# Adapter-conditioned feed-forward layer on one core: the order of the first loads, the bias copy and the steps of side work in the opening stage

## The reference

```python
# conditioning: one low-rank adapter (rank 16) for each of 8 batches, chosen by itok
Bx   = einsum('bni,bri->bnr', x, cond_B[itok])       # x: 8 x 512 x 2048, float32
cond = einsum('bnr,bor->bno', Bx, cond_A[itok])
# feed-forward on cond
base   = einsum('bsi,oi->bso', cond, base_w) + base_b    # base_w: 2048 x 2048
hid    = einsum('bsi,ri->bsr', cond, ffn_A)              # ffn_A: 64 x 2048
probs  = softmax(einsum('bsi,ei->bse', cond, router_w))  # 16 experts
combine = one-hot of the top 2, weighted and normalized
delta  = einsum('bse,bsr,eor->bso', combine, hid, ffn_B) # ffn_B: 16 x 2048 x 64
out = x + base + 0.5 * delta
```

## Time and profile before

| | before |
|---|---|
| median of 3 runs | 472.77 us (472.57 to 473.4) |
| the profiled execution | 471.14 us, of which the span from first to last instruction is 468.9 us |
| TensorE busy | 414.8 us, 88% |
| VectorE busy | 298.5 us, 64% |
| moved by DMA | 135.31 MB, 289 GB/s over the span |
| mean granted TensorE clock | 0.981 of full speed |

### The profile page before, as it was taken

One profiled execution on the slowest core, in us unless ns is written; L12 is line 12 of the kernel. 1 busy time (PEld: TensorE's weight loads), 2 busy tenths in 40 slices (PEclk: granted clock), 3 DMA queues, 4 the chain that ended last, 5 costly groups with the idle time before them and its releaser, 6 DMA issues.

```text
span 468.9 us, 6167 instructions
## 1 busy us (share of the span) xinstructions
PE 414.8 (88%) x2240; PEld 278.2 (59%) x2240; DVE 298.5 (64%) x699; ACT 108.9 (23%) x166; POOL 48.2 (10%) x54
## 2 busy tenths in 40 slices
PE   0056879998988999999999999999999999999996
PEld 0045767777755566566556755655665566566675
DVE  1587249795636666757775677667567766767353
ACT  0011231425543432023002301310230132123210
POOL 3332000001200012002001200120120012002000
PEclk9999778999999999999999999999999999999999
DMA  8999999969997998899889989998997999655844
GB/s 201 202 359 343 353 358 365 297 189 355 296 302 154 271 342 303 290 291 370 293 282 328 335 273 293 369 323 270 293 363 264 293 336 325 241 192 180 300 170 180
DMA packets 97876, 135.31 MB, mean 289 GB/s; under 512 B 14068, under 2 KB 50932, under 8 KB 97844
## 3 DMA queue, kind: packets, MB, share of 16 engines
q1 hardware_dynamic: 67380, 102.07, 66.2%
q10 hardware_dynamic: 30466, 32.84, 24.0%
HBM read 99.24 MB, written 35.65 MB: 288 GB/s over the span
## 4 chain that ended last, share of the span: by engine, by line
PE 70%; DVE 11%; DMA 8%; ACTq 6%; issue 2%; ACT 1%; SPq 0%; DVEq 0%
PE ps L858 13%; PE ps L875 12%; PE ps L876 10%; PE ps L877 10%; PE ps L823 7%; PE ps L888 7%; PE ps L878 5%; DMA bexpT<-in_x 4%; DMA early_u<-in_L_ffn_B 4%; PE ps L813 4%; DVE h_r L673 4%; DVE xT L692 4%; ACTq L293 3%; DVE xbuf L801 2%; ACTq L278 2%
## 5 line engine op out<-in xcount | busy, mean ns | idle before, releaser
L801 DVE TENSOR_TENSOR xbuf<-ps,xbuf 128x512 f32<-128x512 f32 x128 | 86.9, 679 | 105.6 <-PE ps L878 105.3
L875 PE MATMUL ps<-h_r,u_r 128*128 128x512 f32 x256 | 109.3, 427 | 9.2 <-DVE xbuf L801 9.2
L876 PE MATMUL ps<-h_r,u_r 128*128 128x512 f32 x256 | 100.3, 392 | 0.0
L877 PE MATMUL ps<-h_r,u_r 128*128 128x512 f32 x256 | 100.1, 391 | 0.0
L823 PE MATMUL ps<-early 128*128 128x256 f32 x256 | 66.8, 412 | 33.2 <-DVE early L611 28.5
L875 PEld LDWEIGHTS ps<-h_r,u_r 128*128 128x128 f32 x256 | 48.0, 188 | 50.2 <-issue 20.1
L823 PEld LDWEIGHTS ps<-early 128*128 128x128 f32 x256 | 50.8, 207 | 45.4 <-issue 29.7
L692 DVE STREAM_TRANSPOSE xT<-xbuf 128x512 f32<-128x512 f32 x112 | 72.0, 681 | 0.0
L858 PE MATMUL ps<-bexpT,cur 128*32 128x512 f32 x512 | 61.6, 598 | 2.1 <-DVE h_r L673 2.1
L633 DVE STREAM_TRANSPOSE early<-xbuf 128x256 f32<-128x256 f32 x128 | 47.4, 415 | 19.5 <-PE ps L823 11.1
L464 ACT ACTIVATE h_r<-ps 128x512 fp32r<-128x512 f32 x64 | 35.7, 594 | 86.7 <-issue 54.3
(11 more groups left out here) (64 smaller groups left out, 228.5 us busy)
## 6 DMA issues: line engine op xcount, KB each, us to landing
out<-xbuf SPq DMA_DIRECT2D x31, 1024.0 KB, 7.1
xbuf<-in_x SPq DMA_DIRECT2D x30, 1024.0 KB, 7.0
xbuf<-in_x SPq DMA_DIRECT2D x28, 512.0 KB, 8.4
xbuf<-in_x ACTq DMA_DIRECT2D x28, 512.0 KB, 9.5
xbuf<-in_L_ffn_base_w SPq DMA_DIRECT2D x16, 512.0 KB, 13.5
xbuf<-in_L_ffn_base_w ACTq DMA_DIRECT2D x16, 512.0 KB, 12.7
gm_r<-g_hilo SPq DMA_DIRECT2D x128, 32.0 KB, 6.1
early_u<-in_L_ffn_B SPq DMA_DIRECT2D x14, 256.0 KB, 11.3
```

Source lines behind the costliest of these rows:

```text
L801: dve.tensor_tensor(xs, ps[:, ACC + t % 2, :], xs, ALU.add).then_inc(s_out, 1)
L875: pe.matmul(acc, u_r[:, b.q, 0, h, tok_t], hi, start=(h == 0), stop=False)
L876: pe.matmul(acc, u_r[:, b.q, 0, h, tok_t], lo, start=False, stop=False)
L877: pe.matmul(acc, u_r[:, b.q, 1, h, tok_t], hi, start=False, stop=False)
```

## The change

A's loads are put among the four transfers of W's first piece on both queues. GpSimd waits for `take_a`'s last copy before it touches the bias. x of batch 0 is requested behind W's sixth piece and transposed in steps 76 to 98 (two blocks in three steps) instead of 44 to 89 (one block in three). The experts' steps move later, most of all the first four; the late ones go behind tiles 1, 2, 5 and 6 instead of 0, 2, 4 and 6. On both queues W's fifth piece goes ahead of expert group 2.

```diff
-        X_AT = {44 + 3 * j: j for j in range(KD)}
-        BX_AFTER = {66: 4, 92: 8}
-        SLOT_AT = {94: 8, 97: 9, 101: 10, 104: 11, 107: 12, 118: 13, 122: 14}
+        X_AT = {76 + 3 * j // 2: j for j in range(KD)}
+        BX_AFTER = {84: 4, 95: 8}
+        SLOT_AT = {97: 8, 100: 9, 104: 10, 107: 11, 110: 12, 119: 13, 123: 14}
-        E_AT = {20: 0, 26: 1, 34: 2, 40: 3, 52: 4, 60: 5, 70: 6, 78: 7, 95: 8, 102: 9, 109: 10, 117: 11}
-        E_LATE = {0: 12, 2: 13, 4: 14, 6: 15}
+        E_AT = {24: 0, 34: 1, 44: 2, 54: 3, 64: 4, 70: 5, 78: 6, 86: 7, 97: 8, 104: 9, 111: 10, 118: 11}
+        E_LATE = {1: 12, 2: 13, 5: 14, 6: 15}
-        E_FRESH, EIN_AT = 11, 94
-        PIECE_AT, X0_AT = {10: 4, 27: 5, 42: 6, 58: 7}, 26
+        E_FRESH, EIN_AT = 11, 97
+        PIECE_AT, X0_AT = {23: 5, 43: 6, 59: 7}, 29
...
-            load_w(sp, 0, (0, 1))
-            load_cond_a(sp, range(0, NAD // 2))
+            load_cond_a(sp, range(0, 1))
+            load_w(sp, 0, (0,))
+            load_cond_a(sp, range(1, 2))
+            load_w(sp, 0, (1,))
+            load_cond_a(sp, range(2, NAD // 2))
...
+            load_w(sp, 4, (0, 1))
             load_experts(sp, 2, 0)
-            load_w(sp, 4, (0, 1))
+            load_w(sp, 5, (0, 1))
             load_experts(sp, 3, 0)
+            load_x0(sp, (0, 1))
             load_experts(sp, 4, 0)
-            load_x0(sp, (0, 1))
-            load_w(sp, 5, (0, 1))
             load_experts(sp, 5, 0)
...
+            pool.wait_ge(s_a, NB)
             pool.wait_ge(s_bias, 32)
...
-            load_w(act, 0, (2, 3))
-            load_cond_a(act, range(NAD // 2, NAD))
+            load_cond_a(act, range(NAD // 2, NAD // 2 + 1))
+            load_w(act, 0, (2,))
+            load_cond_a(act, range(NAD // 2 + 1, NAD // 2 + 2))
+            load_w(act, 0, (3,))
+            load_cond_a(act, range(NAD // 2 + 2, NAD))
...
             load_experts(act, 1, 1)
+            load_w(act, 4, (2, 3))
             load_experts(act, 2, 1)
```

## The result

The changed kernel takes 479.56 us (median of 4 runs, 478.98 to 479.69) against 472.94 for the kernel before: ratio 1.0137, 95% interval 1.0119 to 1.0155. It is slower by 6.6 us where 3.8 us of gain were forecast. The profiled span is 477.5 us, 8.6 more than before; the profiled execution of the kernel before lay 1.6 us under its median, so differences between these two traces come out up to 2 us larger than those between the medians.

A forecast was written before the change was run, and what follows sets the result against it. It took TensorE as the busiest engine, with DMA feeding the stage up to 80 us. A lead of 3.3 us plus 0.5 from the late experts made 3.8 us: 469.0 us, range 465.0 to 473.9.

The forecast's parts named there:

- Part 1: Opening: GpSimd's bias after A shortens A's copies from 9.1 to 2.3 us; first product at 21.6 instead of 28.45.
- Part 2: A's loads among W's: A still lands at 19.1; 2 us later or earlier would be swallowed by the next wait.
- Part 3: Waits at expert groups 0 and 1: four steps (1.7 us) left of 6.8; TensorE at step 34 at about 47.7.
- Part 4: Steps 34 to 64: step 64 at 76, a lead of 15 steps, 6.5 us.
- its two limits: Step 64: TensorE's path with ScalarE's stand in x's issue until 52.6 gives 75.0; group 4's landing behind x gives 74.8.
- The slower rival: Group 4 lands late behind x and delays everything from step 64, at 82: 2.2 us slower, 475.0; chance 0.20.
- a sign of being wrong: At step 64: the prediction is wrong if expert group 4 lands after 80.
- Part 5: Dense x stretch, steps 76 to 98: VectorE sets it, second x product ends at 101.3, lead falls to 4.5 us.
- Part 6: Steps 97 to 127: logits at step 100 wait 1.2 us behind expert group 8, lead 3.3; the rest counts nothing.
- Part 7: Late experts among the tiles: h ahead of group 12's copy, new stalls between close flips; net gain 0.5 us.
- the real gain: Expert groups 0 and 1: more steps ahead of each load use idle time; step 34 at 47.7, before step 26.

The follow-up runs named there:

- b1: Kernel before with GpSimd's wait for the copies of A (bias after A) as its only change: ratio 0.9993.
- b2: Kernel before with A's loads among W's first piece as its only change: ratio 1.0091.
- a1: Changed kernel with A behind W's first piece again, as before: ratio 1.0083 to the kernel before.
- repaired kernel: Changed kernel with A behind W, the store of g's first part early, the routing earlier and group 5 ahead of W (d3): ratio 0.9968.
- f2: Repaired kernel (d3) with A among W's first piece again: ratio 1.0015.
- c2: Changed kernel with the late experts behind tiles 0, 2, 4 and 6 as before: ratio 1.0171.
- d1: c3 with the routing's parts 8 to 14 one or two steps earlier each: ratio 0.9975.
- f3: Repaired kernel (d3) with the store of g's first part behind expert groups 5 and 6 again: ratio 1.0024.
- c1: Changed kernel with the routing's part 8 at step 96 instead of 97: ratio 1.0145.
- f1: Changed kernel with the routing's parts one or two steps earlier: ratio 1.0102.
- c3: Changed kernel with A behind W and the store of g's first part ahead of expert groups 5 and 6: ratio 1.0028.
- d3: c3 with the routing earlier and expert group 5 ahead of W's seventh piece on ScalarE's queue: ratio 0.9968.
- f4: Kernel before with x requested late and transposed densely, and the routing's steps as in f1: ratio 1.0080.

## Why the prediction was wrong

**Part 1 held.** 1.71 us for the copies, the first product at 21.35 in b1 (21.6 predicted), the transposes at their old speed (14 in 6.08 us in b1, begun beside GpSimd's subtraction, 14 in 6.06 before). One reading was short: line 611 had three stretched copies, not one. Those of 1692 and 1983 ns ran beside the two casts of 1885 and 2042 ns, that of 4583 ns beside the subtraction; the earlier trace rows, which gives least, median and most, does not show the first two.

**Part 2 failed.** "I leave A's landing at 19.1": it moved to 21.7 to 22.1, and expert group 0 to between 42.6 and 43.3. I had let the next wait swallow a late A, but the same delay moves the loads behind A, and so that wait itself. Worth 4.3 us in the kernel before (b2), 2.6 in the changed one (a1), 2.2 in the repaired one (f2). Why A is late was not separated: the windows show 185 instead of 194 GB/s up to 20 us, and ScalarE's issues of A end at 16.14, SyncE's at 13.81, where before the two ended within 0.8 us of each other.

**Part 3 held** where A was not late: in b1 the 7 us are gone at group 0, and a1 has group 1 flipped at 47.86 for 47.7.

**Part 4's sizes were near, but of its two limits only one was met.** With A behind W, step 64 comes at 77.3 (a1) for 76, and group 4 lands at 75.2 for 74.8. TensorE does not wait there for group 4's load (at most 0.26 us, in c2): the time goes to ScalarE's stand in x's issue, as the part also had it. In the changed kernel that stand ends 6 us later than I let it (58.6 for 52.6), in a1 1.6 us later (54.2), so most of it is A's delay again. The slower rival, group 4 behind x, did not happen in its own words, but it came near: in the changed kernel group 4 landed at 81.1, past the 80 that I had named as a sign of being wrong, and 0.9 us before TensorE was there. That step 64 came at 82, the rival's figure, is chance: the stand set it.

**Part 5 failed in one term.** "g's high and low part 1.3" supposed that only the experts' copies hold them up. Line 501 also has them wait for the store of the part before, and I had listed neither that wait nor what stands ahead of the store in SyncE's order: expert group 6's load, whose buffer comes free with the flips that the change moves from step 40 to 54. That is a moved step passing a queue. From the start of step 64's flips to the end of g's low part the part has 5.0 us; the changed kernel needs 8.9 and d1, with the early store, 5.4. Worth 2.6 us in the repaired kernel (f3). The stretch itself took 109.6 - 92.8 = 16.8 us, as summed.

**Part 6 had the wait right (1.15 for 1.2) but not its worth**: c1 took it away and gained nothing (±1.2). Its absolute times also do not follow from part 5's 101.3: it lets the flips end 3.2 us behind the x product, and in the changed kernel they end 1.5 us behind; only the difference of two times entered the sum. What I "counted as nothing", the end of the routing, was a term, and "has its order of before" was wrong: part 14 went from step 122 to 123 and so behind h's first products. Its flips on TensorE follow those of part 13 by 4.2 us instead of 2.2, VectorE and ScalarE wait for them, and u's low part is the last to arrive. TensorE idles 1.1 us longer, and its clock is granted at 0.59 and 0.56 behind that. The routing's earlier steps are worth 1.7 us in the changed kernel (f1), 2.5 in c3 (d1); no run moved part 14 alone.

**Part 7** forecast 0.5 us; the trace shows 0.0, the ratio of c2 1.6 (±1.4).

The three together, A's order, the store and the routing's end, account for 7.7 of the 10.4 us between forecast and result: 1.0137 with all of them, 0.9975 without (d1). Of the other 2.7, d1's trace shows 2.0 at the first addition, where its lead is 1.3 us and not 3.3: 1.1 is gone at the second x product (102.4 for 101.3), and behind it the wait at the logits is absent, but from h's last products before the tiles to the first addition d1 needs 5.4 us and the kernel before 3.8, at granted clocks of 0.59 and 0.56 against 1.00. What is left of the change, 1.2 us faster (1.5 in d3), is the net of more steps ahead of the experts' loads, which the prediction called the real gain, and of x's move, which with the routing's steps loses 3.8 us in the kernel before (f4). How much the experts' new steps alone would win was not tried.

## What to carry to other kernels

When a step moves, walk every in-order queue that issues something behind it, down to the transfers that free a buffer, and list every wait of the instruction that you cost, not only the one that ended last. Look as well at what the step now passes on its own engine: one step, from 122 to 123, put part 14 behind products that it had stood ahead of. The waits that DMA set here gave nothing back for an earlier start ahead of them (b1), but they did not swallow a late start of the queues either (4.3 us in b2, 2.2 in f2), since the delay moves their own loads. A loss that is taken out can in part come back in the next wait: with the store early, the wait for group 5 grew from 1.84 to 3.00 us. So take losses out together as well as singly, and compare medians: c3's one trace, 2.9 us off its median, showed a wait of 4.48 us that the same loads set at 0.84 in d1.

## What the hardware showed beyond the expected

The shared port turned up at a second place. Timeline of the changed kernel's routing:

```profile
118.87 1.26 POOL L446 TENSOR_TENSOR sbx_r<-bx,sbx_r 32x512 fp32r<-32x512 f32 x1 [43.32 <-ACT sbx_r L468]
118.96 1.25 DVE L731 TENSOR_TENSOR ex<-ex,rs 128x64 f32<-128x64 f32 x1
```

VectorE's small multiplication ran 0.23 us before and 1.25 here, from its start up to GpSimd's end. The Trainium skill (SBUF — State Buffer, section "Who interferes with whom") lets an operation with two SBUF inputs block against a GpSimd operation that reads SBUF; the trace agrees.

TensorE's clock did not follow the last idle stretch alone: before, 2.10 us of it were followed by products in 1.92 us at a clock of 1.00; in d1 the same 2.10 us were followed by products in 2.56 us and clocks of 0.59 and 0.56 in the 2 us windows from 130 us on (the 1.2 GHz level for most of them). What else differs was not found.
